# Attention on two heads at once: scores on two row tiles, value sums in one bank, stacks loaded by pairs

## The reference

```
q = x @ Wq;  latent = (x @ Wk + x @ Wv) @ W_down_kv
k = latent @ W_up_k;  v = latent @ W_up_v        # 16 heads of width 8, 2 batches: 32 heads
scores = clip(q k^T * scale) * exp(-0.0001 * |i - j|)     # 1024 x 1024 for each head
out = softmax(scores) @ v;  y = out @ Wo
```

## Time and profile before

| | |
|---|---|
| median of 3 runs | 1056.13 us |
| profiled execution | 1055.84 us |
| its span | 1054.1 us |
| TensorE busy | 1002.5 us (95%) |
| VectorE busy | 809.6 us (77%) |
| ScalarE busy | 789.7 us (75%) |
| GpSimd busy | 236.1 us (22%) |
| mean granted TensorE clock | 0.993 |

### The profile page before, as it was taken

The page is one execution under the profiler, slowest core; times in us unless marked ns, Lnnn a source line. Parts: engine busy times, 40 slices in busy tenths (PEclk is TensorE's granted clock), DMA queues, the critical chain, the costliest instruction groups (busy, mean ns, idle before and its releaser), DMA issues.

```text
span 1054.1 us, 20306 instructions
## 1 busy us (share of the span) xinstructions
PE 1002.5 (95%) x5240; PEld 681.7 (65%) x5272; DVE 809.6 (77%) x1836; ACT 789.7 (75%) x1356; POOL 236.1 (22%) x371
## 2 busy tenths in 40 slices
PE   5799999999997899999999999999998998999997
PEld 3333333333345688888888888888884887788885
DVE  8644444444458699999999999999995788699997
ACT  5789999999977678778788788787785553855554
POOL 3777765544473000000000000000005112300000
PEclk9899999999999999999999999999999999999999
DMA  4478776666660677777777777767731000043321
GB/s 134 145 233 265 241 257 227 229 225 218 222 212 22 213 278 248 244 233 239 242 239 246 246 239 235 240 239 245 239 109 60 1 2 1 1 128 125 117 92 40
DMA packets 102991, 188.98 MB, mean 179 GB/s; under 512 B 11932, under 2 KB 56604, under 8 KB 102940
## 3 DMA queue, kind: packets, MB, share of 16 engines
q1 hardware_dynamic: 102756, 188.19, 54.7%
q10 hardware_dynamic: 192, 0.30, 0.1%
HBM read 152.46 MB, written 35.98 MB: 179 GB/s over the span
## 4 chain that ended last, share of the span: by engine, by line
PE 85%; DVE 5%; ACT 3%; DMA 2%; issue 2%; POOL 1%; SPq 1%; DVEq 0%; ACTq 0%; POOLq 0%
PE bank L1480 28%; PE bank L1493 16%; PE bank L1378 12%; PE bank L1487 8%; PE bank L1359 6%; PE bank L1362 5%; PE bank L1578 1%; PE bank L1389 1%; DVE state L2051 1%; PE bank L1203 1%; DMA c_rows<-fold 1%; POOL rstd L689 1%; PE bank L1588 1%; DVE stats L1702 1%; ACT xn L881 1%
## 5 line engine op out<-in xcount | busy, mean ns | idle before, releaser
L1480 PE MATMUL bank<-xh,w_parts 128*128 128x512 f32 x896 | 276.4, 390 | 2.2 <-ACT xn L1130 1.3
L982 ACT ACTIVATE ring<-bank 128x1024 f32<-128x1024 f32 x256 | 247.4, 1021 | 27.1 <-DVE bank L1857 19.2
L1081 ACT ACTIVATE bank<-bank 128x512 f32<-128x512 f32 x320 | 186.3, 582 | 88.1 <-PE bank L1480 88.1
L1965 DVE TENSOR_TENSOR bank<-bank,ring 128x512 f32<-128x512 f32 x320 | 223.9, 700 | 27.5 <-DMA ring<-c_rows 5.0
L1493 PE MATMUL bank<-hh,w_parts 128*128 128x512 f32 x772 | 238.1, 389 | 0.0
L1957 DVE TENSOR_TENSOR hl<-bank,hh 128x512 fp32r<-128x512 f32 x321 | 218.6, 681 | 0.1
L1075 ACT ACTIVATE hh<-bank 128x512 fp32r<-128x512 f32 x321 | 190.7, 594 | 3.1 <-DVE bank L1965 2.9
L1480 PEld LDWEIGHTS bank<-xh,w_parts 128*128 128x128 f32 x896 | 167.3, 188 | 38.9 <-DVEq L1951 1.7
L1857 DVE TENSOR_TENSOR bank<-bank,corner 128x128 f32<-128x128 f32 x256 | 76.4, 299 | 151.0 <-PE bank L1362 147.2
L1480 PE MATMUL bank<-xl,w_parts 128*128 128x512 f32 x448 | 174.3, 389 | 0.0
L1493 PEld LDWEIGHTS bank<-hh,w_parts 128*128 128x128 f32 x772 | 144.8, 188 | 30.5 <-ACT hh L1075 0.8
(11 more groups left out here) (321 smaller groups left out, 1138.9 us busy)
## 6 DMA issues: line engine op xcount, KB each, us to landing
ring<-c_rows SPq DMA_DIRECT2D x173, 512.0 KB, 4.8
w_parts<-w_pairs SPq DMA_DIRECT2D x160, 128.0 KB, 3.0
w_pairs<-xh SPq DMA_DIRECT2D x16, 768.0 KB, 4.3
q_stack<-q_parts SPq DMA_DIRECT2D x63, 144.0 KB
k_stack<-k_parts SPq DMA_DIRECT2D x189, 48.0 KB
w_pairs<-xl SPq DMA_DIRECT2D x16, 512.0 KB, 2.9
big<-in_w_exp SPq DMA_DIRECT2D x16, 384.0 KB, 4.8
w_ffn_parts<-xl SPq DMA_DIRECT2D x16, 384.0 KB, 3.6
```

The lines of the kernel that those rows point to most:

```text
L982: act.activation(ring[:, c % RING * S:(c % RING + 1) * S], wide[(m + c) % SB][:], ACT.Exp, bias=-BOUND).then_inc(exp_done, 1)
L1081: act.activation(bank(4 + c % ZB), bank(4 + c % ZB), ACT.Silu).then_inc(silu_ready, 1)
L1480: ins = pe.matmul(out_, w[i], x_[j], start=start and k == 0, stop=stop and k == 2, skip_group_check=not start)
L1965: dve.tensor_tensor(bank(4 + c % ZB), bank(4 + c % ZB), cb[u][:, g * GW:(g + 1) * GW], ALU.mult).then_inc(hid_ready, 1)
```

## The change

Two heads of a pair are worked on at once, key tile by key tile. PAIRS becomes 8 (the product of the two smallest parts is left out), so that a head's stack has 64 rows, and `q_stack[s]`, `k_stack[s]` hold both heads: head u in rows 64u to 64u + 63, the two variants side by side in the columns. There are two sets, s = i % 2. `two_scores` issues the matmuls of both heads in turn, each with 64 rows, into two PSUM buffers, and waits once for two tiles. `products` puts both heads' sums into one bank (6 + s), one head in column tiles 0 and 1, the other in 2 and 3, and accumulates over 8 key tiles. So evacuation, transposes and `finish` come once a pair, and `finish` no longer adds. Stacks are loaded for a pair at once, after its last scores, for the pair two later: ten DMAs of 4 KB rows (q: 48 and 16 rows, k: 24, 24 and 16, for each head). The parts of both variants lie in one DRAM tensor. The zeroing of the stacks and the waits on it go. TensorE's and VectorE's loops become two turns of six pairs and four pairs written out. ScalarE's exps and their order in the buffers are unchanged.

```diff
-PAIRS = 9
+PAIRS = 8
+ROWS = PAIRS * HD
...
-        q_stack = [[sb(f"q_stack{s}{u}", [P, S], BF16) for u in range(2)] for s in range(2)]
-        k_stack = [[sb(f"k_stack{s}{u}", [P, S], BF16) for u in range(2)] for s in range(2)]
+        q_stack = [sb(f"q_stack{s}", [P, 2 * S], BF16) for s in range(2)]
+        k_stack = [sb(f"k_stack{s}", [P, 2 * S], BF16) for s in range(2)]
+        def q_rows(s, u, v, lo, hi):
+            return q_stack[s][u * ROWS:(u + 1) * ROWS, v * S + lo:v * S + hi]
...
+        def load_q(eng, n, s, u):
+            for row, rows, first_line, lines, copies in ((0, 48, 0, 16, 3), (48, 16, 16, 8, 2)):
+                eng.dma_start(q_stack[s][u * ROWS + row:u * ROWS + row + rows, :],
+                              bass.AP(q_dram.tensor, n * head_lines + first_line * line, [[line, lines], [0, copies], [1, line]]))\
+                    .then_inc(stacks_loaded[s], 16)
+        def load_k(eng, n, s, u):
+            for i in range(2):
+                eng.dma_start(k_stack[s][u * ROWS + i * 24:u * ROWS + (i + 1) * 24, :],
...
+            eng.dma_start(k_stack[s][u * ROWS + 48:(u + 1) * ROWS, :],
...
-            sp.wait_ge(stacks_zero, 1)
-            load_stacks(0, 0, (0,))
-            load_stacks(1, 1)
+            for u in range(2):
+                load_q(sp, u, 0, u)
+            load_heads(1, 1)
...
+            def next_heads(i, s, scores_done, loads=True):
+                ready(sp, scores_done, i * (2 * QT) + (QT - 1))
+                save_parts(i, 0)
+                load_raw(i + 1, 0)
+                ready(sp, scores_done, i * (2 * QT) + (2 * QT - 1))
+                if loads:
+                    load_heads(i + 2, s)
+                save_parts(i, 1)
+                load_raw(i + 1, 1)
...
+            def two_heads(i, s, late=None, values=True):
+                split_chunk(i, 0)
+                if late:
+                    late_part(late)
+                split_chunk(i, 1)
+                if values:
+                    pool.wait_ge(pv_done, i * (2 * QT) + (2 * QT + RING))
+                    for u in range(2):
+                        take_values(i * 2 + (4 + u), s, u)
...
             act.wait_ge(parts_saved, 2 * 8 * 16)
-            act.wait_ge(stacks_zero, 1)
-            load_stack(act, 0, 0, 1)
+            for u in range(2):
+                load_k(act, u, 0, u)
...
+                def two_scores(j, b, p):
+                    b, k = b + p // QT, p % QT
+                    s, n = b % 2, (j * 6 + b) * (2 * QT) + (2 * k + 1)
+                    if not isinstance(j, int) or j * 6 * QT + b * QT + k:
                         free(pe, exp_done, n, SB)
...
+                    own, at = k // 4, k % 4 * P
+                    def part(u, h, v, lo, hi):
+                        return pe.matmul(wide[(b + 2 * k + u) % SB][:, h * 512 + lo:h * 512 + hi], k_rows(s, u, v, k * P, (k + 1) * P),
+                                         q_rows(s, u, 1 - v, h * 512 + lo, h * 512 + hi), start=True, stop=True)
+                    for u in range(2):
+                        if at:
+                            part(u, own, 0, 0, at)
+                    for u in range(2):
+                        part(u, own, 1, at, 512).then_inc(first_half, 1)
+                    for u in range(2):
+                        part(u, 1 - own, 1 - own, 0, 512).then_inc(whole, 1)
+                def products(j, b, p):
+                    s, i = b % 2, j * 6 + b
+                    ready(pe, exp_done, i * (2 * QT) + (2 * p + 1))
+                    if p == 0:
+                        ready(pe, v_loaded, i * 2 + (1 - CREDIT))
+                        ready(pe, head_ready, i - 1)
+                    for u in range(2):
+                        at_ring = (2 * p + u) % RING * S
                         for h in range(2):
+                            at = 32 * (2 * u + h)
+                            ins = pe.matmul(bank(6 + s)[at:at + 32, :], v_cur[s][u][:, p, :], ring[:, at_ring + h * 512:at_ring + (h + 1) * 512],
+                                            start=(p == 0), stop=(p == QT - 1), skip_group_check=True)
                         ins.then_inc(pv_done, 1)
...
+                def body(j, b, last=False):
+                    for p in range(QT):
+                        if not last or p + 2 < QT:
+                            two_scores(j, b, p + 2)
+                        products(j, b, p)
+                        if p in (2, 4):
+                            turn(j * 6 + b, b % 2, p // 2 - 1)
...
-            for u in range(2):
-                for v in range(2):
-                    for stack in (q_stack, k_stack):
-                        ins = dve.memset(stack[v][u][:], 0.0)
...
+                def diagonal_tiles(j, b, p):
+                    b, k = b + p // QT, p % QT
+                    for u in range(2):
+                        ready(dve, first_half, (j * 6 + b) * (2 * QT) + (2 * k + u))
+                        tile = wide[(b + 2 * k + u) % SB][:, k * P:(k + 1) * P]
+                        dve.tensor_tensor(tile, tile, corner[:], ALU.mult).then_inc(corner_done, 1)
...
+                def body(j, b, last=False):
+                    for p in range(QT):
+                        if not last or p + 2 < QT:
+                            diagonal_tiles(j, b, p + 2)
+                        if p == 0:
+                            evacuate(j * 6 + b, b % 2)
+                        if p in (5, 6):
+                            finish(j * 6 + b, b % 2, p - 5)
```

More of the change, by code:

```diff
@@ L556, in _ @@
             fast = sp.value_load(flag[0:1, 0:1], min_val=0, max_val=1)
[L557 to L563 removed]
+            def next_heads(i, s, scores_done, loads=True):
[7 more added lines that the diff above has]
+                load_raw(i + 1, 1)
             with sp.If(fast == 1):
[L566 to L567 removed]
+                for i in range(6):
+                    next_heads(i, i % 2, whole)
                     if i == 0:
@@ L570, in _ @@
                         store_late(1)
-                    if i < 6:
-                        store_late(i + 2)
+                    store_late(i + 2)
                 sp.wait_ge(late_saved, 2 * 8 * 16)
-                with sp.Fori(7, NH // 2 - 1) as i:
-                    next_heads(i, whole)
+                with sp.Fori(3, 7) as j:
+                    for e in range(2):
+                        next_heads(j * 2 + e, e, whole)
+                next_heads(NH // 2 - 2, 0, whole, False)
             with sp.Else():
@@ L579, in _ @@
                 sp.wait_ge(late_saved, 2 * 8 * 16)
-                with sp.Fori(0, NH // 2 - 1) as i:
-                    next_heads(i, s_psum)
+                with sp.Fori(0, 7) as j:
+                    for e in range(2):
+                        next_heads(j * 2 + e, e, s_psum)
+                next_heads(NH // 2 - 2, 0, s_psum, False)
             for u in range(2):
@@ L1366, in products @@
[L1366 to L1375 removed]
+                        pe.wait_ge(stacks_loaded[s], j * (3 * 160) + 160 * (1 + b // 2))
@@ L1390, in turn @@
                     if half_ == 1:
                         ins.then_inc(evacT_psum, 1)
-                def body(i, m, last):
-                    for c in range(2 * QT):
-                        if not last or c + SB < 2 * QT:
-                            scores(i, c + SB, m)
-                        if c % 2:
-                            products(i, c)
-                        if c % QT in (2, 4):
-                            turn(i * 2 + c // QT, c // QT, c % QT // 2 - 1)
-                for c in range(SB):
-                    scores(0, c, 0)
@@ L1408, in _ @@
+                for p in range(2):
+                    two_scores(0, 0, p)
+                with pe.Fori(0, 2) as j:
+                    for b in range(6):
+                        body(j, b)
+                for b in range(4):
+                    body(2, b, b == 3)
                 turn_heads(0)
@@ L1418, in _, with general @@
                 pe.sem_inc(o_psum, CREDIT)
-                with pe.Fori(0, NH // 2) as i:
+                def general(i, e, pair):
                     for c in range(2 * QT + 2):
@@ L1444, in _ @@
                                 ins = pe.matmul(bank(6 + c % 2)[:, 0:HD], prT[c % 2][:, k * P:(k + 1) * P],
-                                                v_cur[u][:, k, 0:HD], start=(k == 0), stop=(k == QT - 1))
+                                                v_cur[0][u][:, k, 0:HD], start=(k == 0), stop=(k == QT - 1))
                             ins.then_inc(o_psum, 1)
+                with pe.Fori(0, NH // 4) as e:
+                    for pair in range(2):
+                        general(e * 2 + pair, e, pair)
                 turn_heads(0)
```

230 lines of the change are left out of this document (88 added, 142 removed).

## The result

The changed kernel takes 1031.9 us (median of 4 runs, 1029.9 to 1034.3), against 1055.5 before: ratio 0.977, 95% interval 0.975 to 0.979, in which before's run of 1437.4 us is left out. The profiled execution is one of 1033.5 us, with a span of 1031.7.

What follows compares the result with a forecast made beforehand. TensorE bounds the attention stage, ScalarE close behind; 127.5 cycles of 1.87 us make 238.1 instead of 267.1, 29.0 less, with +1.5 for the first load 27.5 less: 1056.1 - 27.5 = 1029 us, range 1021 to 1050.

Steps and rivals of the forecast that it cites:

- The bound and the ceiling: Attention stage: TensorE is the bound; ScalarE's floor of 255 x 0.918 = 234.0 us, 33.1 under now, caps the gain.
- Part 1, the scores: TensorE: two heads' score matmuls run side by side, 0.49 us for two tiles instead of 0.98; plain cycle 1.48.
- rival C: TensorE: matmuls on half the rows hide no weight loads; mean cycle 2.59 us, time 1120 us; chance 0.05.
- Part 2, transposes: TensorE: transposes in two of eight cycles; with form change and open weight load such a cycle takes about 1.95 us.
- the forecast's mean: Attention stage: mean cycle for two tiles, six of 1.84 and two of 1.95 us in eight, 1.87 us.
- Part 3, the chain: Three score buffers: exp to matmul to VectorE's diagonal tile to next exp takes 1.72 us, against 1.84 for two exps.
- the cover: Score buffers: the chain from exp to next pair's exp has 0.12 us to spare against two exps.
- Rival B: Score buffers: the chain through them becomes the bound; cycle 1.92 to 1.97 us, time 1035 to 1041; chance 0.16.
- Part 4: VectorE and GpSimd: their work stays hidden, GpSimd's values being wanted a pair later; cost nothing.
- Part 5, the first load: Stack loads: the first grows from 576 to 1024 KB and costs +1.5 us (bounds -0.5 and +4); later ones hidden.
- the upper bound: First stack load: +4 us, if the second pair's 1 MB gets in between.
- rival D: TensorE: idles enough to fall to the 1.2 GHz level; cycle about 2.8 us; chance 0.02.

Runs made afterwards that it cites:

- e8: The kernel before with 64 instead of 512 score columns in each tile's half away from the diagonal (results wrong), score banks cleared first: 1032.9 us, ratio 0.978.
- e9: The changed kernel with every score matmul over all 128 rows instead of its head's 64 (results wrong): 1056.6 us, ratio 1.000.
- e5: The changed kernel with a 96-column memset on VectorE ahead of the first head's diagonal tile, 128 times: 1039.6 us, ratio 0.984.
- e2: The changed kernel with the second pair's loads issued only when the first pair's have landed: 1029.1 us, ratio 0.975.
- e3: The changed kernel with eight float32 matmuls into an unused bank while TensorE waits for the stacks: 1031.3 us, ratio 0.977.
- e1: The changed kernel with the scores of two tiles issued head after head instead of piece by piece in turn: 1032.6 us, ratio 0.977.

## Why the prediction was right, and where it was off

The forecast was 1029 us, in terms of the profiled execution 1028.3; that execution took 1033.5, the runs' median was 1031.9. Point by point:

- **The bound and the ceiling.** Right. ScalarE's step is 0.92 us in plain cycles, and e8 and e9 show from both sides that TensorE's time held the kernel before. The ceiling of 234.0 us was approached, not reached: 240.6.
- **Part 1, the scores.** Right that they run side by side, shown by e9. The columns stand at half; the chain shows 0.65 from first matmul to last end in a plain cycle, and the products start 0.54 after the first score matmul (186.68, 187.22). That is nearer my 0.49 than the 0.64 worked out from the Trainium skill's gain of 3.07 for four tiles ("TensorE: Matmul & The Clock Gate", Part 3). Its sentence on loads is not borne out here as a cost: on each row group the 0.54 us hold 1024 columns, 0.43 us at 2.4 GHz, and three loads of 95 ns, of which so at most one stood open. Nothing of rival C's price appeared.
- **Part 2, transposes.** Right in effect, off in the split. I had 1.95 for such a cycle, it is 1.90 to 1.91: 0.54 for the scores, 1.00 for the products and 0.37 from the first transpose to the next scores. In that 0.37 the change of form and the open weight load, for which I had added 0.13 and 0.10, come to 0.10 together: the scores start 0.21 us behind the start of the second transpose, and 0.11 in e9, where the form stays 128 rows and the load starts under the transposes. A third cycle of the eight is longer too, by 0.07 to 0.14, the one at the head of a pair: there TensorE waits for the exp and then for the stacks, and the chain shows 0.12 us of issue instead of 0.05; ScalarE's own queue adds up to 0.07 more (0.10 from tile to exp, 183.66 to 183.76, instead of 0.03). A pair took 14.99 us (183.76 to 198.75), 1.874 a cycle; the forecast's mean was 1.8675.
- **Part 3, the chain.** The mechanism was named, the cover was mis-sized: under 0.01 instead of 0.12. I read the 0.95 us from exp to matmul at a place where TensorE had work queued. With TensorE standing still it is 1.08. That it cost nothing was luck: the chain stopped at just the length of two exps, and every further 0.08 us on it would have cost some 8 us (e5). Rival B was this close, and 0.16 was too low for it.
- **Part 4.** Right, for another reason. GpSimd's waits in the stage (total us, times, longest) answer to the earlier trace rows:

```profile
POOL xl L772 <- DMA big<-in_w_ffn: 44.2, 11, 5.8
...
POOL v_first L757 <- PE bank L1416: 17.4, 6, 7.6
...
POOL decay L757 <- PE bank L1416: 8.9, 6, 2.2
```

  It waited 91.1 us for the products, now 26.3, and 44.2 for raw weights, which I hadn't said; that the second chunk's load now stands behind the ten loads of a pair's stacks on SyncE's queue is the likely reason, but no run tests it. GpSimd had the slack, and TensorE's gaps that end on its values are 2.6 us in all.
- **Part 5, the first load.** The step that was most off: 3.7 us instead of 1.5, inside its bounds (up to 4), in two places. e2 shows that 1.0 us is the second pair's, which I had named as the upper bound's reason and put at nothing in the sum. And the 448 KB more did not come at 201 to 301 GB/s: in e2, with the second pair out of the way, the first pair took 8.6 us from the first issue to the last landing (36.42, 44.98) where before took 5.9 (36.01, 41.92), 2.65 more, which is some 170 GB/s. A part of it is ScalarE's queue, which I had called even: in the changed kernel it was done 0.45 us later than before (38.98 against 38.53). Why the rest is that slow was not tested. The Trainium skill ("DMA: Bandwidth & Descriptors", Why a DMA increments its semaphore by 16 and not by 1) says that a DMA uses as many engines, up to 16, as divide the slowest dimension of both its sides; by that the loads of 24 rows go over 12 engines and those of 16 rows, whose source counts 8, over 8. But by the same rule before's loads went over 12 engines as well, and no row here shows the engines one by one, so the cause stays open. The loads during the stage were hidden, as said.
- **The rest.** 2.5 us more in the steps than forecast. 1.6 of it is in the six steps up to the seventh exp (46.86 to 54.08, 7.2 us instead of 5.6), with TensorE at its 1.2 GHz level up to 55 us (0.51 granted at 49 to 55), which I had left out; in e3, with the clock at 1.0 up to 51.8, they took 1.1 less. It is the sign that I had named for rival D, but it was over after four cycles. The other 249 steps took 233.4 us instead of 232.5, 0.9 more, and 1.874 for 1.8675 a cycle accounts for 0.8.

Sum: 2.2 + 2.5 + 0.4 behind the stage = 5.1 us, which is the distance between 1028.3 and 1033.5.

## What to carry to other kernels

When a change relieves the engine that seems full, read the next engine's own pitch from back-to-back instructions: that, times the count, is the ceiling, and here the result came within 3% of it. Then add up the chain through the buffers with latencies taken where the relieved engine stands still, since that is how it will be. And a test that is to undo an overlap must make it impossible, not reorder it. A lower time is no evidence for an edit as long as the part that the edit doesn't touch varies by as much: look for the gain where it should be.

## What the runs showed of the hardware

- Matmuls on different row tiles run as if each tile had a queue of its own: in e1 the fourth matmul of the program ran beside the first (both in flight at 184.42), and the products followed the first score matmul by 0.54 us in both orders.
- An exp's end reached a waiting TensorE 1.08 us after the exp's start, and one with queued work as if at 0.95, 0.07 ahead of the recorded end (187.44 against 187.51).
- A change of the array's form from transposes (128 rows) to scores of 64 rows, with the weight load that it leaves open, took 0.10 us: 0.21 from the last transpose's start to the first score matmul's, against 0.11 with scores of 128 rows (e9).
- The granted clock of the changed kernel stood at 0.5 from 34.5 to 54.9 us. In this stretch lie 7 us without a matmul (38.5 to 45.6); in the last 6 us before the clock rose TensorE was busy 4.87. In e3, with matmuls through the wait, it rose at 41.6 and was at 0.5 again from 51.8 to 55.2.
